# Modulation weights queued at once, four projection banks, background pieces in turn and spaced, casts of the second norm deferred

## The chip, the cores and the metric

The kernel runs on the 8 cores of one Trainium2 chip. Each core works on one batch element; the cores exchange nothing. The metric is the device time in microseconds of the slowest core.

## The reference

One adaLN block: a modulation from `c`, attention over 2048 tokens with 16 heads of 64, and a gated feed-forward with quantised activations and ternary weights. For one batch element:

```python
mod = silu(c) @ wmod                       # 6 vectors of 1024: sa, ca, ga, sb, cb, gb
ga = sign(ga) * max(|ga|, 0.25); gb likewise
h = layernorm(x) * (1 + ca) + sa
x = x + ga * attention(h, W_qkv)
h = layernorm(x) * (1 + cb) + sb
x = x + gb * ffn(h)
# ffn(h) = bit(silu(bit(h, w_gate)) * bit(h, w_up), w_down)
# bit(x, w) = quant127_per_token(x) @ ternary(w), with
# ternary(w) = clip(round(w / mean|w|), -1, 1) * mean|w|
```

Every core has all weights to load and to make ternary itself: w_gate, w_up and w_down are 16 MB each in float32, and each is read twice, once for the mean of |w| and once for the ternary values.

## The kernel before

Each engine has a `Lane`, which runs its instructions in the order of the program text; `need` puts a wait in front of the next one. Loads and stores go out on SyncE's queue (`Y`), except the first constants (ScalarE) and the attention weights (`load_wqk`, `load_wv`, on GpSimd). `V` is VectorE, `S` ScalarE (ACT), `G` GpSimd (POOL).

**Start.** Five constants are loaded on ScalarE's queue, and V, S, PE and G all wait for the last of them. x comes in 16 tiles of 128 tokens, in four blocks n of four. `mod_load(k)` loads a tile of the modulation matrix into one of six buffers, `mod_dot(k)` multiplies it with silu(c) on V and sums it into a column of `modv`; the first 16 columns give `modv` and `avec` (lines 519 to 528). For each block, `stats(n)` takes mean and variance on V, with a square root on S; `normalize(n)` scales on S (block 0) or G; `turn(n)` transposes eight times four tiles on PE into the banks of `psS`, which S (five of eight) and V (three) evacuate into `hA` with scale and bias. `project(n)` makes K of the first head pair and V of the first two: jobs of 8 or 16 matmuls into a bank of `psP`, then a square on S, casts on V, and a small matmul for the norms (lines 531 to 544). `take_bank` hands out the two banks of `psP`.

**Attention.** 512 steps (loop at line 1028): group g of 16 steps is one head pair (c = g // 4) against 512 queries (q = g % 4). A step makes scores (`emit_scores`), their exponentials (`emit_exp`, 128x1024 on S) and, some steps later, the products with V (`emit_av`). `queue_group` adds the projections of the next group or head pair as jobs; `run_jobs` spreads their matmuls over the steps, and a job waits until `BANK_GAP` = 4 steps after the older bank's last end. Odd c below 7 have V projections too. At the end of a group `finish_group`, `divide` and `add_residual` run on V; PE's next group waits for the division at line 743.

**Background.** `bg` holds pieces: `piece_mean(m, k)` loads 128x1024 of a weight matrix (m = 0 gate, 1 up, 2 down) into one of four buffers `stg` and sums |w| on V (line 577); `piece_tern(m, k)` loads it again, scales and clips on G (lines 597, 600) and casts to fp8, on V in attention and on S from step 512 on (lines 618, 621); `piece_mod(k)` is one more dot product. `job_scale(m)` turns the sums into a scale with one small matmul. `bg_tick` is called once a step: it runs the parts that are due (none while a group is being finished), and starts the next piece when it has a credit, fewer than four are under way and the next buffer is free. Order: means of 0 and 1, modulation, ternary 0 and 1, means of 2, ternary 2. The ternary gate and up stay in `tg` and `tu`; that of down goes to the tensor `td` in memory, from which `dt8` is loaded.

**Behind attention.** `norm2_stages(g, wide)` is the second norm with quantisation for 256 tokens, a list of stages; the list for g = 0 runs one stage a step from step 464 on, once no job is left (line 1050). Its first stage loads x2n, stages `cast(0)` and on need it. `emit_A(g)` is the gate and up pass over 16 pairs of tiles: 16 matmuls for the gate, 16 for up, three V and two S instructions; after each pair a hook runs `rate` stages of the next norm and one `bg_tick`. `emit_C(g)` is the down pass. The order is A(0), A(1), C(0), A(2), C(1) and so on.

## Time and profile before

| | us |
|---|---|
| median of the runs shown | 1600.59 |
| profiled execution | 1589.67 |
| its span, slowest core (6) | 1588.1 |
| PE busy | 1392.0 (88%) |
| VectorE busy | 1122.2 (71%) |
| ScalarE busy | 1013.6 (64%) |
| GpSimd busy | 377.9 (24%) |

The spans of the eight cores run from 1579.0 to 1588.1 us. Busy time of PE counts a matmul from start to modelled end, with overlaps taken once; it says that something is on the engine, not that it runs at its peak. The stages matter more than these sums: the start lasts to 128.8 us, attention to 826.6, and from 987.4 on the feed-forward runs in the steady order.

### The profile page before, as it was taken

Reading aid. Unit: us, or ns where it says so; the run is one execution under the profiler, and the core shown is the slowest. Engines: PE = TensorE matmul, PEld = TensorE weight load, DVE = VectorE, ACT = ScalarE, POOL = GpSimd, SP = SyncE. Lnnn points to the kernel's source line nnn. Section 1 sums busy time; section 2 is a strip of 40 time slices with the busy share of each in tenths; the row PEclk is TensorE's granted clock in tenths of the full one; section 3 lists DMA queues with packets and bytes.
Section 4 is the critical chain, followed back from the end, with each engine's and each line's share of the span. In section 5 each row is a group of like instructions: output and inputs, shape, how many; then the busy total and the mean of one; then the engine's idle time right before and its main releaser. Section 6 shows DMA issues by size and latency. Waiting matters only on the chain.

```text
span 1588.1 us, 28129 instructions; the slowest of 8 cores (1579.0 to 1588.1 us)
## 1 busy us (share of the span) xinstructions
PE 1392.0 (88%) x9640; PEld 955.0 (60%) x9702; DVE 1122.2 (71%) x1803; ACT 1013.6 (64%) x1313; POOL 377.9 (24%) x341
## 2 busy tenths in 40 slices
PE   0368989999999899989688596999999999999997
PEld 0243334433544344433247485888898888889885
DVE  3757778788766666578696968768686777777561
ACT  2126867788778777878747378665657475655451
POOL 5411000000336666551026533101000010101011
PEclk9688999999999999999889898999999999999999
DMA  9904655656445545446526355604132140505043
GB/s 244 326 4 146 197 188 161 211 186 225 160 146 168 170 128 158 159 150 218 190 99 183 118 158 159 187 1 142 46 93 95 46 142 13 174 1 160 1 139 115
DMA packets 88364, 222.76 MB, mean 140 GB/s; under 512 B 8480, under 2 KB 37408, under 8 KB 88224
## 3 DMA queue, kind: packets, MB, share of 16 engines
q1 hardware_dynamic: 85776, 214.47, 42.1%
q0 software_dynamic: 1728, 6.29, 2.2%
q8 instruction: 80, 1.31, 0.3%
q14 instruction: 60, 0.49, 0.1%
q10 hardware_dynamic: 720, 0.20, 0.1%
HBM read 206.24 MB, written 20.97 MB: 143 GB/s over the span
## 4 chain that ended last, share of the span: by engine, by line
PE 63%; DVE 18%; DMA 6%; issue 6%; ACT 4%; POOL 2%; DVEq 0%; ACTq 0%; POOLq 0%; SPq 0%
PE psS L1133 13%; PE psV L1264 12%; PE psS L1141 12%; PE psV L747 9%; PE psS L728 8%; PE psP L329 3%; PE psP L391 3%; DVE Dt L759 2%; DVE Dt L767 2%; DMA stg<-wu 2%; DVE macc L577 1%; DMA stg<-wg 1%; DMA wm<-wmodT 1%; DVE Rt L771 1%; DMA b_swap<-bswap 1%
## 5 line engine op out<-in xcount | busy, mean ns | idle before, releaser
L735 ACT ACTIVATE PT<-psS 128x1024 bf16<-128x1024 f32 x512 | 504.4, 1025 | 145.5 <-PE psS L728 140.5
L728 PE MATMUL psS<-Qz,Kz 128*128 128x512 bf16 x989 | 302.3, 385 | 33.4 <-ACT PT L735 25.4
L747 PE MATMUL psV<-PT,Vt 128*128 128x512 bf16 x1006 | 285.2, 384 | 25.5 <-DVE Rt L771 24.3
L1133 PE MATMUL psS<-hq,tg 128*128 128x256 bf16 x2048 | 247.8, 275 | 10.6 <-DVE hq L962 7.3
L1141 PE MATMUL psS<-hq,tu 128*128 128x256 bf16 x2048 | 246.5, 274 | 10.6 <-DVE gup L1107 10.6
L1264 PE MATMUL psV<-gq,dt 128*128 128x256 bf16 x2048 | 234.2, 276 | 17.5 <-DMA dt<-td 12.3
L1264 PEld LDWEIGHTS psV<-gq,dt 128*128 128x128 fp8e4 x2048 | 201.9, 99 | 44.5 <-issue 19.5
L1133 PEld LDWEIGHTS psS<-hq,tg 128*128 128x128 fp8e4 x2048 | 201.7, 99 | 36.0 <-issue 11.4
L1141 PEld LDWEIGHTS psS<-hq,tu 128*128 128x128 fp8e4 x2048 | 200.8, 98 | 36.8 <-issue 12.6
L728 PEld LDWEIGHTS psS<-Qz,Kz 128*128 128x128 bf16 x1024 | 93.2, 98 | 166.3 <-issue 90.3
L747 PEld LDWEIGHTS psV<-PT,Vt 128*128 128x128 bf16 x1024 | 99.8, 99 | 151.6 <-issue 38.4
L1147 DVE TENSOR_TENSOR sg<-psS,alB 128x512 f32<-128x512 f32 x128 | 88.2, 689 | 130.0 <-PE psS L1133 127.4
L1282 POOL TENSOR_TENSOR xo<-xo,ot 128x512 f32<-128x512 f32 x32 | 42.6, 1331 | 564.4 <-DVE ot L1276 564.4
L1152 ACT ACTIVATE sg<-sg 128x512 f32<-128x512 f32 x128 | 79.9, 625 | 149.0 <-DVE sg L1147 148.6
L329 PE MATMUL psP<-hA,wqk 128*128 128x512 bf16 x504 | 147.1, 387 | 5.9 <-DVE Kz L339 2.9
L1219 ACT ACTIVATE vq<-vq,cst_s 128x512 f32<-128x512 f32 x128 | 91.3, 713 | 85.4 <-DVE vq L1214 84.7
L597 POOL TENSOR_SCALAR stg<-stg,mstat 128x1024 f32<-128x1024 f32 x96 | 120.3, 1254 | 102.2 <-DMA stg<-wd 58.1
L375 POOL TENSOR_SCALAR Qz<-yrt,nkm 1x512 bf16<-1x512 f32 x32 | 25.8, 806 | 442.2 <-DVE yrt L369 442.2
L577 DVE TENSOR_REDUCE macc<-stg 128x1 f32<-128x1024 f32 x96 | 113.6, 1213 | 15.0 <-DMA stg<-wg 6.3
L1214 DVE TENSOR_TENSOR vq<-gup,s2B 128x512 f32<-128x512 f32 x128 | 98.0, 772 | 17.3 <-ACT gq L1221 17.1
L600 POOL TENSOR_SCALAR stg<-stg 128x1024 f32<-128x1024 f32 x96 | 106.1, 1105 | 15.9 <-POOL stg L597 15.3
L1221 ACT ACTIVATE gq<-vq,cst_s 128x512 bf16<-128x512 f32 x128 | 92.4, 722 | 12.4 <-ACT vq L1219 0.7
(130 smaller groups left out, 1569.8 us busy)
## 6 DMA issues: line engine op xcount, KB each, us to landing
stg<-wg SPq DMA_DIRECT2D x64, 512.0 KB, 5.0
stg<-wu SPq DMA_DIRECT2D x64, 512.0 KB, 4.9
stg<-wd SPq DMA_DIRECT2D x64, 512.0 KB, 4.5
dt<-td SPq DMA_DIRECT2D x64, 512.0 KB, 4.6
wm<-wmodT SPq DMA_DIRECT2D x48, 512.0 KB, 8.1
xin<-x SPq DMA_DIRECT2D x16, 512.0 KB, 13.0
xr<-xT SPq DMA_DIRECT2D x32, 256.0 KB, 3.1
x2d<-xr SPq DMA_DIRECT2D x32, 256.0 KB, 2.0
```

What stands on the lines that cost most here:

```text
L329: return PE.e.matmul(bank, wt[:, (w * 8 + i) * 128:(w * 8 + i + 1) * 128], hA[:, i * T + n * 512:i * T + (n + 1) * 512], start=(i == 0), s ...
L577: st_free[b] = mean_tok[m] = V.did(V.e.reduce_sum(macc[:, m * 32 + k:m * 32 + k + 1], stg[b], axis=AX, apply_absolute_value=True))
L597: t = G.did(G.e.tensor_scalar(stg[b], stg[b], mstat[:, 4 * m + 1:4 * m + 2], RND, ALU.mult, ALU.add))
L600: st["p1"] = tern_row[0] = G.did(G.e.tensor_scalar(stg[b], stg[b], RND + 1.0, RND - 1.0, ALU.min, ALU.max))
L728: ins = PE.e.matmul(bankS(2 * b + hd), Kz[c % 2][hd][:, kt * 128:(kt + 1) * 128], Qz[g % 3][hd], start=True, stop=True)
L735: exp_tok[s] = s_free[b] = S.did(S.e.activation(PT[s % NPT], psS[:, b * 1024:(b + 1) * 1024], AF.Exp, scale=0.125))
L747: ins = PE.e.matmul((psA, psD)[hd], Vt[c % 3][:, vo:vo + 128], PT[s % NPT][:, hd * 512:(hd + 1) * 512], start=(kt == 0), stop=(kt == 15))
L1133: ins = PE.e.matmul(bankS(b)[:, o_ * 256:(o_ + 1) * 256], tg[:, w:w + 128], hq[g % 2][:, db * 256:(db + 1) * 256], start=(db == 0), stop=( ...
L1141: ins = PE.e.matmul(bankS(2 + b)[:, o_ * 256:(o_ + 1) * 256], tu[:, w:w + 128], hq[g % 2][:, db * 256:(db + 1) * 256], start=(db == 0), st ...
L1214: t = V.did(V.e.tensor_tensor(vq[b].rearrange("p (o t) -> p o t", o=2), gb[:, i * 512:(i + 1) * 512].rearrange("p (o t) -> p o t", o=2), b ...
L1221: ff["vq"][b] = gq_tok[(g, i)] = S.did(S.e.activation(gqb[:, i * 1024:i * 1024 + 512], vq[b], AF.Identity, bias=cst[:, 2:3]))
L1264: ins = PE.e.matmul(bank[:, k * 256:(k + 1) * 256], dt8[wb][:, oc * 128:(oc + 1) * 128], gqb[:, (oc // 2) * 1024 + (oc % 2) * 256: (oc // ...
```

## The change

- Sixteen buffers for modulation tiles instead of six, so the first 16 are all issued ahead; x tiles 4 to 15 are issued right behind them, three of the constants on SyncE's queue between x tiles 7 and 8. Only two constants are loaded on ScalarE's queue, and only S and PE wait for them at the start. `load_wqk(1)` moves behind the memsets, wqk(0) and wv(0) ahead of all but the first memset.
- Up to the first attention step the projections take turns over four banks: the two of `psP`, and `psA` and `psD`.
- `turn(0)` to `turn(2)` are evacuated by ScalarE alone, and `project(0)` stands behind `stats(2)` and `normalize(2)`.
- `bg`: means of 0, modulation, then for m = 0 and 1 ternary tiles of m and means of m + 1 in turn, then ternary 2. A piece starts every second step at the earliest, without credits, with parts 6 and 9 steps after the start (before 9 and 12); none starts in steps 470 to 511.
- `norm2_stages(0, True)` has nine empty stages between load and first cast, five before.
- Three stages of the norm per hook in A(0), two before.

```diff
@@ -123,7 +123,8 @@
     tu = at("tu", o + 32, [128, 32768], FP8)
     xin = [at("xin%d" % i, (o, o, 145, 173)[i // 4] + 16 * (i // 4 == 1) + 4 * (i % 4),
               [128, 1024], F32) for i in range(16)]
-    wm = [at("wm%d" % i, o + 32 + 4 * i, [128, 1024], F32) for i in range(6)]
+    wm = [at("wm%d" % i, o + 32 + 4 * i if i < 6 else 67 + 4 * (i - 6) if i < 14 else
+             (189, 199)[i - 14], [128, 1024], F32) for i in range(16)]
     cB = at("cB", o + 56, [128, 1024], F32)
     mjunk = at("mjunk", o + 60, [128, 1024], F32)
     o = 67
@@ -187,34 +188,38 @@
         return psS[:, i * 512:(i + 1) * 512]
 
     def bankP(i):
+        if i > 1:
+            return (psA, psD)[i - 2]
         return psP[:, i * 512:(i + 1) * 512]
 
...
-    f_c = Flow(nc, "const")
-    for dst, src in [(cst, cst_d), (ident, identf_d), (onesf, onesf_d), (onesb, onesb_d),
-                     (bswap, bswap_d)]:
+    f_c, f_c2 = Flow(nc, "const"), Flow(nc, "const2")
+    for dst, src in [(cst, cst_d), (ident, identf_d)]:
         t_const = f_c.go(S, dst, src)
-    for lane in (V, S, PE, G):
-        lane.need(t_const)
-
-
-    f_wm = [Flow(nc, "wm%d" % i) for i in range(6)]
-    wm_free = [None] * 6
+    S.need(t_const)
+    PE.need(t_const)
+
+
+    f_wm = [Flow(nc, "wm%d" % i) for i in range(16)]
+    wm_free = [None] * 16
     wm_tok = {}
     modt = {}
 
+    def wm_slot(k):
+        return k if k < 16 else k % 6
+
     def mod_load(k):
-        b = k % 6
+        b = wm_slot(k)
         Y.need(wm_free[b])
         wm_tok[k] = f_wm[b].go(Y, wm[b], wmod_d[k * 128:(k + 1) * 128, :])
 
     mj, t_silc = {"t": None}, [None]
 
     def mod_dot(k):
-        b = k % 6
+        b = wm_slot(k)
         V.need(wm_tok[k], t_silc[0], mj["t"])
         t = V.did(V.e.scalar_tensor_tensor(mjunk, wm[b], 1.0, cB, ALU.mult, ALU.mult,
                                            accum_out=modv[:, k:k + 1]))
@@ -239,14 +244,18 @@
     gate_vec_t = [None]
 
 
-    p_free = [None, None]
-    p_end = [-9, -9]
+    p_free = [None] * 4
+    p_end = [-9] * 4
     now = [0]
     p_order = []
+    p_wide = [True, 0, 1, 2, 3]
     p_one = [False]
 
     def take_bank(b=None):
-        if b is None:
+        if p_wide[0]:
+            p_wide.append(p_wide.pop(1))
+            b = p_wide[-1]
+        elif b is None:
             b = 1 if p_one[0] or p_end[1] < p_end[0] else 0
         PE.need(p_free[b])
         return b
@@ -267,7 +276,7 @@
             if job_state["cur"] is None:
                 if not jobs:
                     return used
-                if budget < 1e6 and now[0] - min(p_end) < BANK_GAP:
+                if budget < 1e6 and now[0] - min(p_end[:2]) < BANK_GAP:
                     return used
                 n, needs, mm, after = jobs.popleft()
                 needs()
@@ -406,10 +415,10 @@
             return t
         job(16, needs, mm, after, 8.0)
 
+    G.did(G.e.memset(Vt[0], 1.0))
     load_wqk(0)
     load_wv(0)
-    load_wqk(1)
-    for i in range(3):
+    for i in range(1, 3):
         G.did(G.e.memset(Vt[i], 1.0))
     for i in range(3):
         for h in range(2):
@@ -432,8 +441,14 @@
     for t in range(4):
         x_load(t)
     t_cB = Flow(nc, "cB").go(Y, cB, bass.AP(c_d.tensor, 0, [[0, 128], [1, D]]))
-    for k in range(6):
+    for k in range(16):
         mod_load(k)
+    for t in range(4, 8):
+        x_load(t)
+    for dst, src in [(onesb, onesb_d), (bswap, bswap_d), (onesf, onesf_d)]:
+        t_const2 = f_c2.go(Y, dst, src)
+    for t in range(8, 16):
+        x_load(t)
     S.need(t_cB)
     t_silc[0] = S.did(S.e.activation(cB, cB, AF.Silu))
     bankS_free = [None] * 4
@@ -485,7 +500,7 @@
...
-            if db % 2 or db == 4:
+            if db in on_act[n]:
...
     turned, ready = {}, {}
+    on_act = (range(8), range(8), range(8), (1, 3, 4, 5, 7))
 
     def project(n):
         PE.need(*ready[n])
         norm_k = job_qk(0, 1, n)
         if n:
+            PE.need(t_const2)
             norms.pop()()
         job_v(0, 2 * n)
         if n < 3:
@@ -519,21 +536,17 @@
     normalize(0)
     for k in range(16):
         mod_dot(k)
-        if k < 10:
-            mod_load(k + 6)
-        elif k == 10:
-            for t in range(4, 16):
-                x_load(t)
     V.need(modt[15])
     t_avec = V.did(V.e.tensor_scalar(avec, modv[:, 8:16], 1.0, None, ALU.add))
     for k in range(16, 22):
         mod_load(k)
+    load_wqk(1)
     turn(0)
     stats(1)
     normalize(1)
-    project(0)
     stats(2)
     normalize(2)
+    project(0)
     turn(1)
     stats(3)
     normalize(3)
@@ -542,6 +555,9 @@
     turn(3)
     project(2)
     project(3)
+    p_wide[0] = False
+    PE.need(t_const2)
+    V.need(t_const, t_const2)
     x_done = turned[3]
 
     LAST = 32 * 16
@@ -665,26 +681,25 @@
 
     vb_tok = [None]
     gv_tok = {}
-    for m in range(2):
-        for k in range(32):
-            bg.append(piece_mean(m, k))
+
+    for k in range(32):
+        bg.append(piece_mean(0, k))
     bg.append((lambda: None, [lambda: sum_rows(0), lambda: job_scale(0)]))
     for k in range(24, 48):
         bg.append(piece_mod(k))
-    bg.append((lambda: None, [lambda: sum_rows(1), vec_b, lambda: job_scale(1)]))
-    for m in range(2):
+    bg.append((lambda: None, [vec_b]))
+    for m in range(3):
         for k in range(32):
             bg.append(piece_tern(m, k))
-    for k in range(32):
-        bg.append(piece_mean(2, k))
-    bg.append((lambda: None, [lambda: sum_rows(2), lambda: job_scale(2)]))
-    for k in range(32):
-        bg.append(piece_tern(2, k))
+            if m < 2:
+                bg.append(piece_mean(m + 1, k))
+        if m < 2:
+            bg.append((lambda: None, [lambda m=m: sum_rows(m + 1), lambda m=m: job_scale(m + 1)]))
     later = deque()
     rest, rest_end = deque(), [-9]
-    under, credit, ahead = [0], [0], [7]
-
-    def bg_tick(step, start=None):
+    under, next_start = [0], [0]
+
+    def bg_tick(step, lead):
 
         quiet = not rest and step > rest_end[0] + 1
         for _ in range(len(later)):
@@ -693,16 +708,15 @@
                 under[0] -= last
             else:
                 later.append((when, part, last))
-        if start:
-            credit[0] += 1
-            ahead[0] = start
-        if credit[0] and bg and under[0] < 4 and not st_held[st_n[0] % 4]:
-            credit[0] -= 1
+        if LAST - 42 <= step < LAST:
+            return
+        if bg and under[0] < 4 and step >= next_start[0] and not st_held[st_n[0] % 4]:
+            next_start[0] = step + (2 if len(bg[0][1]) < 2 else 2)
             under[0] += 1
             load, parts = bg.popleft()
             load()
             for i, part in enumerate(parts):
-                later.append((step + ahead[0] + 3 * i, part, i == len(parts) - 1))
+                later.append((step + lead + 3 * i, part, i == len(parts) - 1))
 
 
     f_xr = [Flow(nc, "xr%d" % i) for i in range(2)]
@@ -740,7 +754,7 @@
         g, kt = s // 16, s % 16
         c = g // 4
         if kt == 0:
-            PE.need(av_free[0])
+            PE.need(av_free[0], p_free[2], p_free[3])
         PE.need(exp_tok[s], v_tok[(c, kt // 2)])
         for hd in range(2):
             vo = (kt * 2 + hd) * 128
@@ -971,7 +985,7 @@
 
         wait = lambda: None
         if wide:
-            return ([load, wait, wait, wait, wait, wait, cast(0), cast(1), wait,
+            return ([load] + [wait] * (9 if g == 0 else 5) + [cast(0), cast(1), wait,
                      both(stat(0), cast(2)), both(stat(1), cast(3)), wait, stat(2), stat(3), wait,
                      var, root, recip] +
                     [both(times(j), minus(j)) for j in range(4)] +
@@ -1054,7 +1068,7 @@
                 side.extend(norm2_stages(0, True))
             if side:
                 side.popleft()()
-        bg_tick(s, 9 if (s % 16) in ((0, 2, 4, 7, 9, 11, 13) if s < 470 else ()) else None)
+        bg_tick(s, 6)
         step += 1
     while rest:
         rest.popleft()()
@@ -1294,7 +1308,7 @@
         run_side(rate[0])
         if bg or later:
             hook_n[0] += 3
-            bg_tick(step + hook_n[0], 4 if bg else None)
+            bg_tick(step + hook_n[0], 4)
             run_jobs(1e9)
 
     hook_n = [0]
@@ -1307,7 +1321,7 @@
         return nxt
 
     side.extend(norm2_stages(1, True))
-    rate = [2]
+    rate = [3]
     emit_A(0, hook_A)
     rate[0] = 1
     drain(side)
```

## Rows read from the trace of the kernel before

**Rows 1.** Start in stages: length; busy PE, PEld, DVE, ACT, POOL; PEclk, DMA, GB/s

```profile
4.00:16.00 12.00, 0.00 (x0) 0.00 (x0) 0.00 (x0) 0.00 (x0) 0.00 (x0) 1.00 0.95 235
16.00:48.00 32.00, 3.64 (x16) 3.27 (x16) 21.88 (x39) 8.56 (x8) 28.93 (x20) 0.85 1.01 290
48.00:79.00 31.00, 15.06 (x83) 11.39 (x84) 22.46 (x48) 7.09 (x12) 8.05 (x8) 0.72 1.01 326
79.00:127.00 48.00, 30.84 (x201) 22.61 (x203) 26.57 (x52) 11.34 (x17) 8.04 (x7) 0.89 0.02 6
```

**Rows 2.** Timeline of the start: start, length, engine, line, instruction, idle before it

```profile
4.03 39.85 SPq L58 DMA_DIRECT2D wm<-wmodT  x16
...
51.39 1.23 DVE L219 SCALAR_TENSOR_TENSOR mjunk<-wm,cB 128x1024 f32<-128x1024 f32 x1 [0.46 <-DMA wm<-wmodT]
...
52.73 0.17 DVE L528 TENSOR_SCALAR avec<-modv 128x8 f32<-128x8 f32 x1
```

**Rows 3.** Timeline, from the statistics of block 3 to the first scores

```profile
86.62 0.30 ACT L456 ACTIVATE rstd<-bnm,cst_s 128x4 f32<-128x4 f32 x1 [5.67 <-DVE bnm L451]
...
96.73 3.65 PE L391 MATMUL psP<-wv,hA 128*128 128x256 bf16 x32 [2.13 <-DVE Kz L339]
...
128.81 1.86 PE L728 MATMUL psS<-Qz,Kz 128*128 128x512 bf16 x4 [4.32 <-POOL Qz L378]
```

**Rows 4.** Stages of attention: three chunks of four groups each, then the last three groups

```profile
220.30:311.40 91.10, 85.94 (x448) 43.55 (x456) 73.63 (x95) 66.79 (x73) 6.58 (x10) 1.00 0.56 173
391.10:481.20 90.10, 85.35 (x449) 43.95 (x456) 63.74 (x102) 66.68 (x73) 32.51 (x29) 1.00 0.43 147
561.20:651.60 90.40, 85.91 (x448) 43.36 (x454) 57.18 (x88) 66.47 (x73) 55.62 (x52) 1.00 0.49 151
751.80:827.70 75.90, 53.79 (x223) 22.45 (x228) 58.75 (x79) 50.75 (x57) 11.52 (x10) 0.87 0.49 161
```

**Rows 5.** Timeline around the second norm's load and the end of attention

```profile
762.63 0.38 SPq L58 DMA_DIRECT2D x2n<-x2d  x1
...
773.01 0.63 ACT L813 ACTIVATE lb<-x2n 128x512 bf16<-128x512 f32 x1 [6.59 <-DMA x2n<-x2d]
...
809.38 1.01 PE L747 MATMUL psV<-PT,Vt 128*128 128x512 bf16 x2 [4.10 <-DVE Rt L771]
...
826.44 1.91 PE L1133 MATMUL psS<-hq,tg 128*128 128x256 bf16 x16
...
836.97 3.30 PE L1133 MATMUL psS<-hq,tg 128*128 128x256 bf16 x16 [3.24 <-DVE mstat L651]
```

**Rows 6.** Stages of A(0) and of a later stretch, and timeline rows between

```profile
826.40:911.90 85.50, 63.62 (x541) 54.12 (x540) 66.59 (x111) 43.91 (x60) 46.31 (x38) 0.92 0.46 139
...
911.94 3.57 PE L1133 MATMUL psS<-hq,tg 128*128 128x256 bf16 x16 [7.03 <-DVE hq L962]
...
987.37 7.24 PE L1264 MATMUL psV<-gq,dt 128*128 128x256 bf16 x48 [12.28 <-DMA dt<-td]
...
1100.00:1150.00 50.00, 50.00 (x461) 44.81 (x459) 35.96 (x59) 36.25 (x56) 2.54 (x2) 1.00 0.28 91
```

**Rows 7.** Groups by line, shapes apart: busy us, mean ns of one, idle before

```profile
L1147 DVE TENSOR_TENSOR sg<-psS,alB 128x512 f32<-128x512 f32 x128 | 88.2, 689 | 130.0 <-PE psS L1133 127.4 <-DMA x2d<-xr 1.7
...
L618 ACT ACTIVATE tdo<-stg,cst_s 128x1024 fp8e4<-128x1024 f32 x32 | 36.3, 1134 | 1.0 <-POOL stg L600 1.0
...
L577 DVE TENSOR_REDUCE macc<-stg 128x1 f32<-128x1024 f32 x96 | 113.6, 1213 | 15.0 <-DMA stg<-wg 6.3 <-DMA stg<-wd 4.0 <-DMA stg<-wu 3.9
...
L490 ACT ACTIVATE hA<-psS,modv,avec 128x512 bf16<-128x512 f32 x20 | 14.9, 773 | 34.5 <-DVE avec L528 22.2 <-PE psS L484 12.0
```

**Rows 8.** Landing of stg loads, 180 to 200 and 600 to 700 us; timeline, group's end

```profile
DMA to landing us min/median/max: 4.3/8.1/10.9
...
DMA to landing us min/median/max: 3.4/4.3/5.5
...
204.01 1.01 PE L747 MATMUL psV<-PT,Vt 128*128 128x512 bf16 x2 [4.84 <-DVE Rt L771]
```

## Prediction

> **What bounds the kernel now.** I read three things in order: the table of stages, then the rows of time inside each stage that is not dense, then the groups by line for prices. The reader should see four stretches.
>
> Start, 0 to 128.8 us: the 16 DMA engines are full from 4 to 79 us and idle afterwards, while PE does only 49.6 us of work in the 123 us shown [rows 1]. The last of the 16 dot products of modulation starts at 51.39 behind its load, and `avec` is there at 52.73 [rows 2]. From there a serial walk goes on: ACT waits 5.67 us for the statistics of block 3 of x, PE waits 2.13 us for a square and two casts before it gets a projection bank, and the first scores come at 128.81 [rows 3].
>
> Attention, 128.8 to 826.6: for three chunks of four groups with V projections the time is 91.1, 90.1 and 90.4 us, with PE busy 85 to 86 of them and Vector at 73.6, 63.7 and 57.2 [rows 4]. The three have different background work (means only, modulation, ternary tiles), so its kind hardly matters there; PE sets the pace. The last three groups are different: 75.9 us with PE at 53.8 and ACT at 50.8, neither full [rows 4].
>
> From the end of attention to the first down-projection, 826.6 to 987.4: A(0), the first up and gate pass, takes until 911.94, 85.5 us for 16 pairs of gate and up tile of 32 matmuls each, which at the later pace of 461 matmuls in 50 us are 3.5 us a pair and 56 in all; A(1) ends 63.2 us later, at 975.1, and PE waits 12.28 us for `dt` [rows 5, 6]. After that PE has hardly a gap, and the change doesn't touch it.
>
> **The change, part by part.**
>
> *Weights of modulation queued at once, fewer constants waited for.* The issue of 16 loads was stretched over 39.85 us, since only six buffers existed [rows 2]. But the DMA engines were full all the time [rows 1], so only the order of bytes can gain. Before `avec` the kernel must load 4 tiles of x, cB, 16 tiles of weights, wqk(0), wv and wqk(1) (Pool issues it behind its memsets, still well before the end): 24 tiles of 0.52 MB, 12.6. The rows moved 12 x 0.235 + 32 x 0.290 = 12.1 MB from 4 to 48. So the last weight tile could land at 49, and it landed at about 51.3, because loads of x ran beside it [rows 1, 2]. Now more loads queue behind it than before, so some of this stays. I take 2 us (0 to 3): `avec` at 50.7. That Vector no longer waits for the constants is worth nothing by itself: its dots end behind their loads, and this covers some ten microseconds of earlier start. In a sentence apart: the Trainium skill, page "DMA: Bandwidth & Descriptors", section "Issuing engines are not separate DMA queues", says that transfers of all issuing engines interleave on the same 16 engines; by it alone the weights gain nothing from being queued early and this term is 0. The full share of 1.01 agrees.
>
> *Turns of blocks 0 to 2 on ACT alone, project(0) behind stats(2).* Eight evacuations x 0.77 = 6 us a block [rows 7], much as long as now, but Vector is free to go on. The new walk: stats(1) ends at about 57.5 (x tile 7 lands at about 56: 2.1 MB after the weights at 0.326 MB/us [rows 1]); stats(2) at 64 (x tile 11 at 62.5); the square, casts and V copies of project(0), twice PE's 2.13, to 68.2; stats(3), which took the 5.67 that ACT waited and a little more, to 74.2 [rows 3]. So the square root of block 3 is at 74.3, where it is at 86.62 now [rows 3]. That is 33.9 us after `avec` now and 23.6 then: 10.3 us. If x lands 3 us later this falls by 3.
>
> *Four banks for projections.* From the root at 86.62 to the first scores takes 42.2 us now [rows 3]. Each of projects 1 to 3 waits once for the casts (2.13) and once more for V's copies or the norm. With psA and psD as third and fourth bank, PE runs project(1) in 8 (the clock is low there), turn(3) in 4, project(2) in 5.7, and project(3) down to the scores in 13, after 4 us in which turn(2) is evacuated: 34.7 us, a gain of 7.5 (4 to 9). First scores at 128.8 - 2 - 10.3 - 7.5 = 109. Start in all: 20, bounds 11 to 25.
>
> *Background order and spacing.* Before, seven starts in 16 steps with nine steps of lead; now one every two steps with six, at most four under way. A mean holds its buffer 6 steps and a ternary tile 9, and nothing runs in 3 steps of 16 around a group's end. By counting, the first 32 means and 24 dots end at about step 118, and each alternating run of 64 takes some 171 steps (6 and 6 in 32): 290, 461. Four ternary tiles of wd fit before step 470, so 28 stay for after attention; now it is all 32 (every one ran on ACT [rows 7]). Costs: 96 means x 1.213 on Vector are unchanged, four ternary casts more, none dearer than a mean: 5 us at most on Vector, which is not the bound. Since three kinds of load gave 90.1 to 91.1, I take 0, cover being Vector's idle 17 to 33 us of 90 [rows 4]. Without that cover they cost their 5. The shorter lead is 6 x 1.36 = 8 us against a landing of 4.3 us in the quiet and 8.1 in the crowded stretch [rows 8]: some waits near the start, so bounds from 8 lost to 3 gained. Apart: the Trainium skill, page "SBUF — State Buffer", section "Who interferes with whom", says that DVE in a two-port mode, or with two SBUF inputs against a reading GpSimd op, waits for GpSimd's whole instruction, and a tensor_reduce never does; so means beside ternary work are the harmless pairing and the term would be 0 or better.
>
> *Nothing started in steps 470 to 511, casts deferred.* Of the 75.9 us of the last three groups ACT, the fullest but Vector, worked 50.8, the floor [rows 4]. The x2n load issued at 762.63 landed at 773.01 and ACT stood 6.59 us before its cast; PE stood 4.10 for Vector at 809.38 [rows 5]. Four more empty steps are 4.4 us, and without stg loads beside it the x2n load lands sooner: the 6.6 goes. About 17 means, 20 us of the 58.8 of Vector, go from this stretch [rows 4, 7], and with them most of the 4.1. GpSimd's chain of eight ops of the norm stays, and Vector waits for it in order. So 75.9 - 6.6 - 3.4 = 66, a gain of 10 (5 to 14).
>
> *What is late next.* The job of scale(2) now falls at step 472 and the bank gap pushes the last norm of Q, and with it the norm's start, from 472 to 475; with four more stages the last stage is at 475 + 41 = 516, past the last step 513. So `spread` and `scale` run behind the last group's division: hq(0) is ready about 11 us after the last AV: the division, for which PE waited 4.84 elsewhere [rows 8], and ten more Vector ops of at most 0.69 [rows 7]. Now PE starts A(0) at once (826.44) but, two tiles on, stands until 836.97, 10.4 us after [rows 5]. Then it starts at 11 with nothing done: 7 us of matmul lost.
>
> *Rate 3 in A(0).* 38 stages at two a hook are 19 hooks, but A(0) has 16; six stages run after it, and PE waits 7.03 us for hq(1) [rows 6]. At three they end in hook 13. A(0)'s Vector work: busy 66.6 of the 85.5 us [rows 6], of which 16 pairs x 3 ops x 0.69 = 33, the last group and mean 10, so the norm 23. It gets heavy at hook 5, when PE has done six pairs, 11 + 21 = 32 us after the last AV; left are 23 + 10.5 x 2.1 + 2 for the root = 47, to 79, and PE ends its tiles about 3 before. So A(1) begins at 76 against 85.3 (911.9 - 826.6): gain 9 (2 to 13), the 7 lost already in it.
>
> *After A(0).* No slow clock at A(1)'s first tiles (3.57 for 16 matmuls, at the later pace 1.74 [rows 6]): 2. The last ternary tile is 3 hooks earlier (28 for 31), 3 x 3.5 = 10 us, so `dt` is there; what is left is the quantised input, freed of three to four ACT casts of 1.13 [rows 7]: 4 (1 to 7).
>
> **Sum.** 20 + 0 + 10 + 9 + 2 + 4 = 45. The profiled execution took 1589.7 (span 1588.1, 1.6 around it), so 1545 by its own clock; the median of the shown runs is 1600.6, 11 above it, so 1556.
>
> **Rivals.**
> A, *the DMA engines bound the start anyway.* For: full to 79 us [rows 1]. Against: 76 us of the start lie behind `avec`, and the engines' loads are over 50 us before its end. If x lands 8 us late in stats(1) to (3), the start gives 12: 1564. The skill's rule above is its reason.
> B, *the deferral only moves the wait.* For: hq(0) comes 11 us late, PE's clock falls (16 matmuls in 3.57 after such a gap), A(0) is Vector-bound. If A(0) regains nothing (0 for 9) and the last groups give 5: 1570.
> C, *the shorter lead.* Vector and Pool work in order, so a mean that waits for its load holds the casts and the division behind it, and PE waits for both. Where the median landing was 8.1 us, at 8 us the lead is just gone [rows 8]. PE waited 4.84 us at the end of a group there [rows 8]. It decides from 10 of the 29 groups (48 us: no gain left); with all of them it is 140 us and 1696, slower. Against: in the rest landing is near half the lead.
>
> **How the numbers follow.** Forecast 0.62, A 0.15, B 0.17, C 0.06. About 2% (32 us, the line at 1568.6) is what a measurement of this kernel tells from no change. The forecast lies on the faster side for 0.58 and within for 0.04; A 0.11 and 0.04; B 0.05 and 0.12; C 0.02 within and 0.04 slower. Faster 0.74, same 0.22, slower 0.04. The range takes A and B in and the high bounds of start, last groups and A(0) in part: 1536 to 1582.
>
> **What would show it.** First scores near 109 (A: 117); `avec` near 50.7; chunks of four groups still at 90 to 91; the last three groups at 66; first tile of A(0) about 11 us behind the last AV and A(1) at 76 behind it; no wait on `dt`; 28 ternary casts on ACT. I am wrong if the groups themselves get slower, most likely with DVE or POOL waiting for stg, or if the ACT-only turns hold PE longer than 6 us a block.

## The result, and the profile after

The changed kernel takes 1590.1 us (median of all executions), the kernel before 1599.6: ratio 0.994, 95% interval 0.9917 to 0.9963. It is 10 us faster, not 45; within 2%, and above the predicted range of 1536 to 1582. (Some executions run up to 12% longer, with the cores of a die at a lower granted clock; the ratios, and the times given further down, leave them out.) The profiled execution took 1600.5 (span 1598.9, core 1) and is the longest of those compared, while that of the kernel before, 1589.7, is shorter than the others of its kernel. So the two profiles overstate what was lost; by how much is worked out below.

The start, in the timeline of core 1 (columns as in [rows 2]):

```profile
52.20 0.17 DVE L540 TENSOR_SCALAR avec<-modv 128x8 f32<-128x8 f32 x1
...
76.19 0.30 ACT L471 ACTIVATE rstd<-bnm,cst_s 128x4 f32<-128x4 f32 x1 [3.75 <-DVE bnm L466]
...
109.70 1.86 PE L742 MATMUL psS<-Qz,Kz 128*128 128x512 bf16 x4 [5.09 <-POOL Qz L387]
```

Against [rows 2, 3]: `avec` 0.5 us earlier, the root of block 3 10.4, the first scores 19.1 (128.81 to 109.70). These are core 6 before and core 1 now; in the mean over the eight cores `avec` stands at 51.9 before and 52.1 now, so it gains nothing, and the first scores at 128.9 and 108.8. The start as a whole did what was forecast.

Attention in stages of the same core (columns as in [rows 4]); each stage runs from one group's end to that of the fourth behind it:

```profile
134.98:238.22 103.24, 83.31 (x362) 35.23 (x360) 74.59 (x94) 66.52 (x73) 6.00 (x9) 0.93 0.65 188
238.22:332.56 94.34, 86.25 (x429) 41.45 (x428) 72.02 (x112) 66.71 (x72) 19.38 (x20) 0.98 0.57 181
...
596.34:682.62 86.28, 82.71 (x424) 40.28 (x423) 63.18 (x88) 66.61 (x73) 33.41 (x33) 1.00 0.51 168
...
761.23:831.47 70.24, 54.50 (x219) 21.04 (x218) 38.99 (x57) 52.42 (x59) 25.34 (x21) 0.88 0.20 64
```

The first stage is 103.24 us long, with VectorE, ScalarE and GpSimd hardly busier than in the kernel before, where core 6 needed:

```profile
153.76:242.70 88.94, 79.09 (x357) 34.85 (x363) 69.21 (x83) 66.54 (x73) 6.00 (x9) 0.96 0.61 190
```

From group 1 to 28 the changed kernel takes 606 to 626 us on its cores, the one before 591 to 598. Here most of the start's gain went, and slower groups are the first sign of being wrong that the prediction names. The waits of core 1 from 135 to 761 us (us in total, times, longest) say behind what:

```profile
POOL stg L613 <- DMA stg<-wg: 64.8, 29, 8.7
POOL stg L613 <- DMA stg<-wu: 53.6, 25, 7.0
...
DVE macc L593 <- DMA stg<-wu: 30.4, 16, 5.6
...
PE psV L761 <- DVE Rt L785: 24.4, 15, 4.4
...
DVE macc L593 <- DMA stg<-wd: 19.4, 10, 7.4
...
DVE macc L593 <- DMA stg<-wg: 17.3, 5, 6.6
```

VectorE's means wait 67.1 us for their loads; in the kernel before, on core 6 from 154 to 752 us, it was 10.6, and 10.2 of it stand in two rows:

```profile
DVE macc L577 <- DMA stg<-wg: 6.3, 4, 2.7
...
DVE macc L577 <- DMA stg<-wu: 3.9, 4, 1.9
```

One chain of such a wait, in the timeline of core 2; first SyncE's queue, then the engines:

```profile
130.35 2.91 SPq L58 DMA_DIRECT2D stg<-wg  x2
139.60 0.33 SPq L58 DMA_DIRECT2D x2d<-xr  x1
142.06 0.33 SPq L58 DMA_DIRECT2D xr<-xT  x1
142.80 15.42 SPq L58 DMA_DIRECT2D stg<-wg  x8
```

```profile
151.05 1.22 DVE L593 TENSOR_REDUCE macc<-stg 128x1 f32<-128x1024 f32 x1 [5.29 <-DMA stg<-wg]
152.31 0.69 DVE L378 TENSOR_SCALAR yrt<-psP 128x512 int32<-128x512 int32 x1
...
153.22 0.69 POOL L384 TENSOR_SCALAR Qz<-yrt,nkm 1x512 bf16<-1x512 f32 x1 [22.29 <-DVE yrt L378]
154.08 0.69 POOL L387 TENSOR_SCALAR Qz<-yrt,nkm 1x512 bf16<-1x512 f32 x1 [0.17 <-POOL Qz L384]
...
154.91 1.01 PE L742 MATMUL psS<-Qz,Kz 128*128 128x512 bf16 x2 [5.24 <-POOL Qz L387]
```

The mean at 151.05 waits 5.29 us for its load, which was issued at 142.80 and landed 8.2 us later. It was also issued late: SyncE's queue took nothing from 133.26 to 139.60, because the store of the residual `x2d` stood at its head and `xr` was not yet there (it is made at the group's end), and from 139.93 to 141.98 the reload of `xr` waited for that store to land. Then four loads of `stg` went out within 1.6 us. Behind it on VectorE stands the root `yrt` for the norm of Q; behind that GpSimd's two ops, and behind those the next group's scores: PE waits 5.24 us. The two matmuls then take 1.01 us where two take 0.59 elsewhere in this stage: the granted clock is 0.50 from 154.9 to 160 us, where it was 1.00 from 144 to 149. Rival C's chain, as it was described; the stall of the queue ahead of it was not in the prediction. Its own waits on core 2 from 135 to 715 us (total, times, longest):

```profile
SPq L46 <- DVE xr L793: 214.6, 26, 13.9
...
SPq L46 <- DMA x2d<-xr: 54.2, 26, 4.0
```

Between the ends of groups 0 and 28 core 2 has 31 waits of over 0.5 us of a mean for its load, 74 us in all. Every one is for a load issued within 5 us behind a wait for such a store to land. The kernel before has the same two waits (core 6: 210.4 and 50.7 us); with nine steps of lead its means wait the 10.6 us above.

Behind attention, core 1 (the last product with V ends at 831.37):

```profile
841.89 0.37 SPq L58 DMA_DIRECT2D x2n<-x2d  x1
...
841.96 3.57 PE L1147 MATMUL psS<-hq,tg 128*128 128x256 bf16 x16 [9.71 <-DVE gtmp L233]
...
989.93 4.83 PE L1278 MATMUL psV<-gq,dt 128*128 128x256 bf16 x22 [4.60 <-DMA dt<-td]
...
996.57 0.38 PE L1278 MATMUL psV<-gq,dt 128*128 128x256 bf16 x2 [1.05 <-ACT gq L1235]
```

A(0) starts 10.6 us behind the last product, as forecast; A(1) starts at 922.5, 91 behind it (85.3 before, 76 forecast); `dt` costs 4.6 instead of 12.3 [rows 6], after which PE waits several times for the quantised input.

### The profile page after: what moved, and what is told of

Its sections match the earlier page's. It is cut to its first block, busy times and chain, and to the rows that moved or that the text cites. A ratio compares the mean times of both kernels' runs of the same rounds, so it can differ in the third digit from the quotient of the medians.

```text
span 1598.9 us, 28123 instructions; the slowest of 8 cores (1576.9 to 1598.9 us)
## 1 busy us (share of the span) xinstructions
PE 1413.7 (88%) x9702; PEld 959.1 (60%) x9702; DVE 1115.0 (70%) x1798; ACT 1014.9 (63%) x1318; POOL 374.4 (23%) x341
## 4 chain that ended last, share of the span: by engine, by line
PE 60%; DVE 17%; DMA 9%; issue 6%; SPq 4%; ACT 3%; POOL 1%; DVEq 0%; POOLq 0%; ACTq 0%
PE psS L1147 12%; PE psV L1278 12%; PE psS L1155 12%; PE psV L761 8%; PE psS L742 7%; SPq L58 3%; DMA stg<-wu 3%; PE psP L338 2%; PE psP L400 2%; DVE Dt L773 2%; DVE Dt L781 2%; DMA stg<-wg 2%; DMA x2d<-xr 2%; DMA wm<-wmodT 1%; DVE Rt L785 1%
## 5 line engine op out<-in xcount | busy, mean ns | idle before, releaser
L742 PE MATMUL psS<-Qz,Kz 128*128 128x512 bf16 x1024 | 314.9, 391 | 28.8 <-ACT PT L749 17.0
L761 PE MATMUL psV<-PT,Vt 128*128 128x512 bf16 x1024 | 292.4, 389 | 29.7 <-DVE Rt L785 29.7
L1278 PE MATMUL psV<-gq,dt 128*128 128x256 bf16 x2048 | 237.5, 277 | 14.0 <-ACT gq L1235 9.4
L1147 PEld LDWEIGHTS psS<-hq,tg 128*128 128x128 fp8e4 x2048 | 201.5, 98 | 34.9 <-issue 10.4
L613 POOL TENSOR_SCALAR stg<-stg,mstat 128x1024 f32<-128x1024 f32 x96 | 116.8, 1216 | 220.0 <-DMA stg<-wd 89.8
L338 PE MATMUL psP<-hA,wqk 128*128 128x512 bf16 x480 | 141.0, 388 | 4.6 <-DVE Kz L348 3.5
(145 smaller groups left out, 1576.3 us busy)
```

The source lines that it names most:

```text
L338: return PE.e.matmul(bank, wt[:, (w * 8 + i) * 128:(w * 8 + i + 1) * 128], hA[:, i * T + n * 512:i * T + (n + 1) * 512], start=(i == 0), s ...
L613: t = G.did(G.e.tensor_scalar(stg[b], stg[b], mstat[:, 4 * m + 1:4 * m + 2], RND, ALU.mult, ALU.add))
L742: ins = PE.e.matmul(bankS(2 * b + hd), Kz[c % 2][hd][:, kt * 128:(kt + 1) * 128], Qz[g % 3][hd], start=True, stop=True)
L761: ins = PE.e.matmul((psA, psD)[hd], Vt[c % 3][:, vo:vo + 128], PT[s % NPT][:, hd * 512:(hd + 1) * 512], start=(kt == 0), stop=(kt == 15))
L1147: ins = PE.e.matmul(bankS(b)[:, o_ * 256:(o_ + 1) * 256], tg[:, w:w + 128], hq[g % 2][:, db * 256:(db + 1) * 256], start=(db == 0), stop=( ...
L1278: ins = PE.e.matmul(bank[:, k * 256:(k + 1) * 256], dt8[wb][:, oc * 128:(oc + 1) * 128], gqb[:, (oc // 2) * 1024 + (oc % 2) * 256: (oc // ...
```

## The experiments

All kernels in one table. Each figure is the mean over the eight cores of the profiled execution: the end of group 0 (start of its first transpose `Dt<-psV`), the time from there to the end of group 28, from there to the end of group 31, and what follows to the end of the span. The ratio is that of the times to those of the kernel before, with its 95% interval; where a time stands instead, there was one execution to go by.

| kernel | group 0 ends | groups 1–28 | last three | behind | ratio |
|---|---|---|---|---|---|
| before | 153.5 | 594.2 | 74.3 | 761.4 | 1 |
| changed | 134.3 | 615.5 | 69.9 | 767.1 | 0.994 (0.992–0.996) |
| start only | 132.2 | 598.0 | 74.5 | 762.8 | 0.986 (0.984–0.989) |
| old background | 133.1 | 596.5 | 71.8 | 761.8 | 0.984 (0.982–0.987) |
| new order, old pace | 132.6 | 582.8 | 71.7 | 798.4 | 1.002 (1.000–1.003) |
| old order, new pace | 132.6 | 648.0 | 70.9 | 755.4 | 1.015 (1.012–1.017) |
| new order, old pace, lead 6 | 132.8 | 627.1 | 82.1 | 756.3 | 1.007 (1.004–1.010) |
| changed, lead 8 | 133.1 | 584.6 | 67.7 | 806.2 | 1600.5 us |
| changed, small loads | 132.9 | 582.7 | 69.9 | 766.3 | 1561.3 us |
| changed, no deferral | 133.8 | 605.5 | 78.4 | 756.0 | 0.992 (0.991–0.994) |
| changed, stop at 462 | 133.7 | 610.4 | 65.3 | 765.9 | 0.995 (0.992–0.998) |
| start only, rate 3 | 132.6 | 595.9 | 74.1 | 757.8 | 0.988 (0.979–0.996) |
| lead 8, gap 2 | 134.1 | 605.3 | 72.6 | 762.2 | 0.991 (0.989–0.994) |
| old background, lead 8, gap 2 | 133.2 | 618.4 | 85.3 | 749.4 | 0.998 (0.996–0.999) |
| start only, two banks | 144.1 | 596.0 | 73.8 | 762.0 | 1587.1 us |
| start only, early project(0) | 141.3 | 595.6 | 74.2 | 761.9 | 1584.0 us |
| lead 8, two a pair | 133.2 | 581.4 | 67.7 | 785.9 | 0.990 (0.987–0.993) |
| lead 7, two a pair | 131.9 | 590.3 | 66.8 | 767.3 | 0.980 (0.978–0.983) |
| new order, old pace, two a pair | 132.6 | 583.8 | 72.9 | 767.3 | 0.981 (0.978–0.984) |
| the same, no deferral | 132.1 | 583.0 | 78.0 | 761.8 | 0.983 (0.978–0.988) |

Two of these, "no deferral" and "stop at 462", run the changed kernel's own code up to step 461, and their groups took 605.5 and 610.4. The five kernels with the background of before and the new start have 595.6 to 598.0, 596.4 in the mean. So against the background of before the changed kernel loses 9 to 19 us in its groups, from run to run.

The groups don't all hold the same work. Loads into `stg` issued between the ends of groups 0 and 28: 138 in the kernel before and with its background; 154 in the changed kernel, without deferral and with small loads (153 with the stop at 462); with the new order 132 at the old pace and 160 at the old pattern with lead 6; 138 with lead 8, 147 to 149 with lead 7; 169 with the old order at the new pace; 149 and 158 in the two kernels with gap 2.

**Start, pace and order.** First the start alone, the changed kernel with background, deferral and rate of before:

```diff
-            return ([load] + [wait] * (9 if g == 0 else 5) + [cast(0), cast(1), wait,
+            return ([load] + [wait] * (5 if g == 0 else 5) + [cast(0), cast(1), wait,
-    rate = [3]
+    rate = [2]
```

(`bg` and `bg_tick` as in the kernel before.)

> The kernel before with the changed start alone (sixteen weight buffers, four banks, turns on ACT, later project(0)); the background's order and pace, the five empty stages and two stages a hook are those of before. The changed kernel reaches its first group's end 17 to 23 us earlier, but its groups 1 to 28 take 9 to 36 us more than before. If the background (pace or order) costs those, this kernel keeps the start's 20 us: about 1580, ratio 0.987, groups 1 to 28 at 591 to 598 us. If the earlier start itself stretches attention, whatever the background (all loads of eight cores fall together differently), the groups take 600 or more here too and the time is 1590 to 1595.

Measured: 1576.3 us, groups 598.0 (595 to 603). The start keeps its 21 us; the background costs most of them in the changed kernel.

The same with nine empty stages and rate 3:

> The changed kernel with the background's order and pace of before (credits, nine steps of lead, no stop at 470); the nine empty stages and three stages a hook stay. Against the start alone it tells what the deferral and the rate are worth. If the deferral and the rate are worth what was forecast for them (10 + 9 less the 17 means that go on beside the last groups), it is some 10 us under the start alone: 1570. If the late hq(0) eats them, as the changed kernel's 205.9 to 198.8 us from last product with V to A(2) suggests (193.4 before), it is level with the start alone or up to 5 us slower: 1578 to 1585.

(The figure 205.9 in it is a slip; the changed kernel's is 198.8.) Ratio 0.984 against 0.986: the last groups give 2.7 us, what follows 1.0, and the intervals overlap. Then order and pace crossed; the pace of before in the new order (`bg_tick` again as in the kernel before):

```diff
-        bg_tick(s, 6)
+        bg_tick(s, 9 if (s % 16) in ((0, 2, 4, 7, 9, 11, 13) if s < 470 else ()) else None)
```

> The changed kernel's order of pieces (means of 0, modulation, then ternary and means in turn) with the pace of before: seven starts in 16 steps, nine steps of lead, no stop at 470. Theory 1 (the shorter lead and the spacing cost the groups): attention is back, groups 1 to 28 at 591 to 598 us, the time 1575 to 1582. Theory 2 (ternary tiles and means in turn cost it, by two kinds of load and two engines on four buffers): groups at 605 to 625 us, the time about 1590.

and the new pace with the old list of pieces:

> The changed kernel with the order of pieces of before, but its own pace: one start every two steps, six steps of lead, none in steps 470 to 511. Theory 1 (lead and spacing): groups 1 to 28 at 605 to 625 us, the time about 1590. Theory 2 (order): groups at 591 to 598 us, the time 1575 to 1582. If both cost a part, this and the kernel with new order and old pace lie between, at about 1585 each.

New order with old pace has the groups at 582.8, new pace with old order at 648.0, over the 605 to 625 expected. So the pace costs them and the order does not: at the same pace the new order takes 14 us less than the old (582.8 for 596.5), with VectorE waiting some 23 us for GpSimd instead of some 30. The gain isn't only a matter of fewer pieces, since the kernel with small loads (below) has 154 loads for 138 and 582.7 us; what makes it isn't shown. In time the first kernel missed its 1575 to 1582 us (ratio 1.002), for it pays behind attention: 36 pieces were left, the scale of matrix 2 came late, and PE waits for `dt`:

```profile
PE psV L1279 <- DMA dt<-td: 42.9, 2, 40.3
```

**Lead or pattern.** The pace has two parts. Eight steps of lead in the changed kernel, and six in the pattern of before:

> The changed kernel with eight steps of lead for six; a start every second step, order and stop as changed. Only attention is to be read: fewer pieces end in it, about 41 are left for behind it, so dt comes late and the whole time is over 1600. If the lead costs the groups, groups 1 to 28 are at 577 to 592 us as with the pace of before, and VectorE's waits for stg are under 20 us; if the pattern (a start every second step) costs them, they stay at 605 or more.

> The changed kernel's order with the start pattern of before (seven in 16 steps, credits) but six steps of lead; about 14 ternary tiles of the last matrix are left for behind attention. If the lead alone costs the groups: groups 1 to 28 at 605 or more, and the time 1585 to 1595. If the pattern costs them: 577 to 592 and, since dt is ready in time, a time of 1560 to 1570, under every kernel so far.

Six steps of lead cost in either pattern (627.1 against 582.8; the time, 1607.7, is over what either theory said), eight in the new one cost nothing (584.6). That speaks for the lead and against the pattern. But these pairs alone don't part the lead from the amount of work, since a shorter lead frees the buffers sooner and lets more loads into the groups (160 for 132, 154 for 138); the small loads below do. And VectorE's waits were not under the 20 us expected at eight steps; they are 34.7 in all on core 0:

```profile
DVE macc L593 <- DMA stg<-wu: 19.3, 7, 5.0
...
DVE macc L593 <- DMA stg<-wd: 8.6, 5, 3.8
...
DVE macc L593 <- DMA stg<-wg: 6.8, 4, 3.2
```

So a wait of this kind is not paid one for one; VectorE has idle time to put it in. Seven steps, with two starts a pair behind attention (below):

> The changed kernel with seven steps of lead and two starts a pair behind attention. Groups 1 to 28 took 605 to 615 us at six steps (three profiled executions) and 581 to 585 at eight. If the cost sets in only where the lead falls under the landing plus the time by which the buffers come free late, seven steps lie near eight: 584 to 592. If it grows evenly with each step taken away: 595 to 600. Some 31 pieces instead of 41 are left behind attention, so the rest is 765 to 775 instead of 786; time 1560 to 1572 in the first case, 1575 to 1582 in the second.

Groups at 590.3 (587 to 594): 583 at eight, 590 at seven, 605 to 616 at six. The cost grows faster than the lead shrinks, as in the first of the two cases expected.

**Landing, or engines.** Is it the late load or the number of operations? All loads into `stg` but the first four bring 64 columns:

```diff
-            st["t"] = f_st[b].go(Y, stg[b], src[:, k * 1024:(k + 1) * 1024])
+            w = 1024 if st_n[0] <= 4 else 64
+            st["t"] = f_st[b].go(Y, stg[b][:, :w], src[:, k * 1024:k * 1024 + w])
```

> The changed kernel in which all loads of weight tiles into stg but the first four bring only 64 of 1024 columns; every VectorE, GpSimd and ScalarE operation stays. It leaves out most of the weights (means and ternary values are of old data). The loads land sooner, so: if late landing behind a six-step lead is what costs attention, groups 1 to 28 fall from 606 to 626 to 575 to 590 us. If it is two engines meeting on the same memory or the number of operations in a group, they stay over 600.

582.7 us with every operation in place and all 154 loads issued. Landings of `stg` from 400 to 580 us, in the changed kernel and then in this one, and this one's waits:

```profile
DMA to landing us min/median/max: 3.5/6.2/10.6
```

```profile
DMA to landing us min/median/max: 1.6/2.2/4.4
...
DVE macc L594 <- DMA stg<-wd: 1.8, 1, 1.8
DVE macc L594 <- DMA stg<-wu: 0.8, 1, 0.8
```

The late landing is the cause, and neither the number of operations nor two engines on the same memory. (The kernel with new order and old pace has full loads, 132 of them, and the same 582.8 us, so it isn't the traffic as such.) The median of 6.2 lies under the 8.2 us of six steps; the upper end does not, and the lead has to cover the load's time in SyncE's queue as well. That time is the same with small loads (core 3: 240.5 us of waits for `xr`), which land soon enough behind it. No run takes the residual off this queue.

**Buffers.** `stg` is held for lead + 3 steps by a ternary tile. With eight steps, two between its parts, and a stop at 476, no deferral:

```diff
-                later.append((step + lead + 3 * i, part, i == len(parts) - 1))
+                later.append((step + lead + 2 * i, part, i == len(parts) - 1))
```

> The changed kernel with eight steps of lead, two steps instead of three between the two parts of a ternary tile (so that a buffer is held 10 steps, not 11), no start in steps 476 to 511 instead of 470 to 511, and five empty stages. If the lead is what costs the groups and the deferral what costs behind attention: groups 1 to 28 at 582 to 592 us (before: 594, changed: 616 in the profiled execution), the rest behind attention at 756 to 764, time 1555 to 1570, under every kernel so far. If the shorter gap makes VectorE wait for GpSimd instead, the groups are at 600 or more and the time at 1575 or more.

> The start changed, order and start pattern of before, but eight steps of lead for nine and two steps between the parts of a ternary tile; five empty stages, three stages a hook. More pieces end inside attention: about 13 ternary tiles are left for 32. If eight steps are enough, groups 1 to 28 stay at 595 to 603 and the rest behind attention falls from 762 to 756 (as in the kernels with 18 tiles left or fewer): time 1565 to 1572. If the edge already lies between eight and nine steps in this order (many pieces in a row of one kind, up to four under way), the groups are at 610 or more and the time at 1580 or more.

The second has the background of before, with the same lead and gap. Both lost: 605.3 and 618.4. VectorE hardly waits for loads of means now (10.8 us on core 4 of the first), but for GpSimd, whose two operations end too late for a cast two steps on. First the changed kernel's core 1, then this one's core 4:

```profile
DVE tu L637 <- POOL stg L616: 4.2, 4, 2.9
...
DVE tg L637 <- POOL stg L616: 0.7, 1, 0.7
```

```profile
DVE tg L637 <- POOL stg L616: 29.7, 10, 4.4
...
DVE tu L637 <- POOL stg L616: 23.4, 10, 4.3
```

The same chain, with another slack taken away. The old order's 648.0 at the new pace has both: on the slowest core VectorE waited 32.5 us for loads of means, 52.8 for GpSimd (17.8 of it before casts of the last matrix) and 6.1 for stores of `td`. Its groups also hold fifteen ternary tiles more than the changed kernel's. How the 32 us between the two kernels fall to these isn't settled.

**The last three groups.** The changed kernel without its four extra empty stages:

```diff
-            return ([load] + [wait] * (9 if g == 0 else 5) + [cast(0), cast(1), wait,
+            return ([load] + [wait] * (5 if g == 0 else 5) + [cast(0), cast(1), wait,
```

> The changed kernel with five empty stages instead of nine before the first cast of the second norm; all else as changed. If the deferral only moves the wait: hq(0) is ready earlier, the first tile of A(0) starts about 2 us behind the last product with V instead of 10.6, the last three groups take 73 instead of 70, and the time stays at 1588 to 1592. If the deferral pays, as forecast, through the last groups: it is 4 to 8 us slower. If it is only a loss through the late hq(0): it is 3 to 7 us faster, 1583 to 1587.

78.4 us for the last groups, 8.5 more than with the deferral (73 were expected), and 4 more than in the kernel before, although no piece is started beside them; behind attention 11.1 us less. Two things make the norm late. Its load is handed out at step 475 instead of 472, as the prediction says under "What is late next": without the deferral ScalarE has begun 482 exponentials before the first cast, in the kernel before 479. Three steps are some 4 us. The rest is in SyncE's queue. The kernel before issues the load 10.9 us behind the end of group 28 (751.75 to 762.63, [rows 5]); in the changed kernel (core 1, group 28 ends at 761.23):

```profile
774.54 6.15 SPq L58 DMA_DIRECT2D td<-tdo  x3
...
780.85 0.38 SPq L58 DMA_DIRECT2D x2n<-x2d  x1
...
786.58 0.63 ACT L827 ACTIVATE lb<-x2n 128x512 bf16<-128x512 f32 x1 [2.98 <-DMA x2n<-x2d]
```

Three stores of ternary tiles stand ahead of it, each waiting for its cast: the load goes out 19.6 us behind the end of group 28, 8.7 later than before, of which some 4 are the later step. The four empty stages only make up for both. A stop eight steps earlier (`LAST - 50`):

> The changed kernel with no start in steps 462 to 511 instead of 470 to 511, so that no ternary tile of the last matrix falls into attention and no store of one stands in SyncE's queue ahead of the second norm's load. If those stores are what kept the load late (issued 19.6 us behind the end of group 28 in the changed kernel, 10.9 before): it is issued at some 11, no wait of ScalarE for it, and the last three groups take 65 to 67 us for 69.9; behind attention 32 tiles are left, which costs 3 to 8 us there, so the time is 1588 to 1594. If the load is late for another reason, the last three groups stay at 69 to 71.

Last groups 65.3 us, as expected, though not by the whole of the mechanism: two stores still stand ahead of the load, which goes out 16.7 us behind the end of group 28 (753.15), 5.8 later than before, some 4 of it again the later step. That is just early enough; ScalarE waits 0.56 for it:

```profile
766.46 3.22 SPq L58 DMA_DIRECT2D td<-tdo  x2
769.84 0.38 SPq L58 DMA_DIRECT2D x2n<-x2d  x1
...
776.09 0.63 ACT L827 ACTIVATE lb<-x2n 128x512 bf16<-128x512 f32 x1 [0.56 <-DMA x2n<-x2d]
```

No time is gained in all (0.995); the 4.6 us are less than the groups before them vary, and the rest stays at 765.9, where 3 to 8 us more were expected for 32 tiles left (30 were cast behind attention).

**Rate.** The start alone, with three stages a hook:

> The start changed, background of before, five empty stages, three stages a hook in A(0) (the kernel with the start alone has two, the one with the deferral nine empty stages and three). The forecast gave rate and hq(0) together 9 us. If the rate alone is worth the gap before A(1) (7 us in the kernel before): the rest is at 754 to 758 us against 762.8, the time 1568 to 1572. If A(0) is bound by VectorE, so that the stages only come earlier and push the gate and up work back: rest 761 to 764, time 1576.

The rest falls from 762.8 to 757.8: with hq(0) in time, rate 3 is worth 5 us in this pair of profiles, as forecast; the times, 1570.1 for 1576.3, agree, though one of the four executions took 1586.8.

**The start's parts.** Two banks (`p_wide` false from the beginning), and `project(0)` ahead of `stats(2)` with turns shared by ScalarE and VectorE:

> The kernel with the changed start alone, but projections before the first step take turns over two banks, as before. The forecast gave four banks 7.5 us (4 to 9): the end of the first group then falls back from 132.2 us (mean of the cores) to 136 to 141. If the walk to the root of block 3 and not the banks sets the first scores, it stays at 132 to 134.

> The kernel with the changed start alone, but project(0) ahead of stats(2) and the turns shared by ACT and VectorE as before. The forecast gave this step 10.3 us together with the weights queued at once: the end of the first group falls back from 132.2 to 139 to 142 us, and the root of block 3 from 76 to some 83 us. If the gain came from the earlier loads of x alone, both stay within 2 us.

Group 0 ends 11.9 us later with two banks (144.1, where 136 to 141 was expected) and 9.1 with the early project(0). First scores and root of block 3 on the slowest cores, two banks and then early project:

```profile
79.62 0.30 ACT L471 ACTIVATE rstd<-bnm,cst_s 128x4 f32<-128x4 f32 x1 [0.67 <-DVE bnm L466]
...
119.51 1.87 PE L745 MATMUL psS<-Qz,Kz 128*128 128x512 bf16 x4 [4.33 <-POOL Qz L387]
```

```profile
83.93 0.30 ACT L471 ACTIVATE rstd<-bnm,cst_s 128x4 f32<-128x4 f32 x1 [5.37 <-DVE bnm L466]
...
117.82 1.87 PE L745 MATMUL psS<-Qz,Kz 128*128 128x512 bf16 x4 [5.09 <-POOL Qz L387]
```

**Keeping both gains.** New order and old pace had the shortest groups and a late `dt`. Two calls of `bg_tick` at each pair of A(0) and A(1), in that kernel and in the changed one with lead 8:

> New order with the pace of before (groups 1 to 28 at 582.8 us, but 798 us behind attention, since dt came 41 us late), now with two calls of bg_tick at each pair of A(0) and A(1). If the ternary tiles behind attention are held back by one start a pair and not by GpSimd or ScalarE, dt is some 25 to 35 us earlier, the rest 765 to 772 us and the time 1560 to 1567, under every kernel so far. If the four buffers or GpSimd hold them back, the rest stays over 785 and the time at 1585 or more.

> The changed kernel with eight steps of lead and two starts at each pair in A(0) and A(1). With eight steps alone the groups took 584.6 us, the last three 67.7, the rest 806. By the same reasoning as in the kernel with new order, pace of before and two a pair: the rest falls by 25 to 35 to 771 to 781 and the time is 1564 to 1574; 1595 or more if buffers or GpSimd are the limit.

The first gives 1565.6 us; its wait for `dt` is 8.5 us (42.9 without). The second keeps 26.7 of it and misses its 771 to 781 by 5: 41 pieces were left there. Lead 7 with two a pair, whose expectation stands above, gave 1565.7. The first without deferral:

> New order, pace of before, two starts a pair, and five empty stages for nine. Against the same kernel with nine stages (last three groups 72.9, rest 767.3) it tells what the deferral does where no store of a ternary tile stands ahead of the norm's load. If the deferral is a trade of a wait in attention for one behind it, the last three groups are 2 to 4 us longer and the rest 4 to 10 shorter, the time 1560 to 1566. If it is a pure gain or loss: 1570, or 1555.

Last groups 5.1 longer, the rest 5.5 shorter: an even trade. Its time, 1569.6, isn't the 1560 to 1566 expected of a trade, but not told apart from the 1565.6 with deferral. The two best, lead 7 and new order with old pace, both with two a pair, are 2.0 and 1.9% under the kernel before and some 1.3% under the changed one.

## Why the prediction was wrong

*Start, 20 us: right.* 19.2 at the end of group 0, as a mean over the cores. Within it, on the two cores compared, `avec` gave 0.5 for 2 (nothing in the mean over the cores); the walk to the root 9.9 for 10.3 (86.62 - 52.73 to 76.19 - 52.20); the banks from root to first scores 8.7 for 7.5 (42.2 to 33.5). Taken back alone, the banks cost 11.9 at the end of group 0, since with two of them the root is 3 us later as well. The Trainium skill, page "DMA: Bandwidth & Descriptors", section "Issuing engines are not separate DMA queues", says that transfers of all issuing engines interleave on the same 16 engines, which gave 0 for the weights; the means of 51.9 and 52.1 us for `avec` agree with it. (Two slips in the working: PE's work in [rows 1] adds up to 49.5 us, not 49.6, and the upper bounds of the three terms, 3, 10.3 and 9, make 22 and not 25.)

Of the forecast's 45 us some 35 are missing. 9 to 19 are lost in the groups, 5.6 in the last three, and 20.7 behind attention, where 9 + 2 + 4 were expected and 5.7 were lost.

*Background, 0 us, bounds 8 lost and 3 gained: the first step that failed.* It cost 9 to 19 us in groups 1 to 28. That is a difference of two effects: against the new order with its loads in time (582.7) the short lead cost 23 to 33 us, and the new order gave some 14 back. I named the mechanism (rival C) and put it at the edge: "at 8 us the lead is just gone" where the median landing was 8.1, and "in the rest landing is near half the lead". Two things were missing. The lead is counted from the step at which a piece is handed out, not from the issue of its load, and SyncE's queue also carries the residual: at each group's end it stands until `xr` is made and until its store has landed (214.6 and 54.2 us on core 2), and loads handed out meanwhile go out late and together. And a load must land in nearly all cases, not in the median one: 3.5 to 10.6 us around a median of 6.2. My own bound was also inconsistent: C at 48 us for 10 groups in the rivals, 8 us in the term's range, and nothing between, though the 23 to 33 us of the lead are what five to seven of 29 groups would give. "Its kind hardly matters" did not hold: at the old pace the new order's groups are 14 us shorter. The Trainium skill, page "SBUF — State Buffer", section "Who interferes with whom", by which a `tensor_reduce` never waits for GpSimd and means beside ternary work are harmless, agrees with 582.7 and 582.8 us.

*Last three groups, 10 us: 4.4.* The size was near what there was to win (9.0 with the stop at 462), but the sum said "without stg loads beside it the x2n load lands sooner" and had not asked what the four ternary tiles that now fit before step 470 bring with them: three stores in the queue ahead of that load. I had counted the four, and priced them at four casts. The three steps by which the norm starts later I had seen too, but they stand in no term of this sum.

*A(0) to A(1), 9 us: the second step that failed, -6 (91 for 76).* The first tile at 11 us was right. hq(1) was ready at 84.5 us behind the last product for 79 forecast. Wrong is "PE ends its tiles about 3 before": the norm ends in hook 13, and pairs 14 to 16 come behind that. Its stages, and VectorE's load with them, fall on the second half:

```profile
841.96:882.00 40.04, 36.14 (x288) 30.24 (x288) 21.30 (x35) 21.24 (x30) 14.16 (x12) 0.88 0.42 136
882.00:922.52 40.52, 30.77 (x250) 25.54 (x251) 37.13 (x63) 18.74 (x26) 17.54 (x14) 0.92 0.37 114
```

VectorE is busy 21 of the first 40 us and 37 of the next 40.5. The norm's first stage, the load of `x2n`, can't go out before hq(0) has left that buffer: issued at 841.89. So the late hq(0) delays twice, and rival B had the mechanism: the rest is 11.1 us shorter without the deferral, and the deferral moves a wait. (B's A(0) was to regain nothing; it lost 6.) With hq(0) in time the rate gave 5. That leaves some 10 of the 20.7 us for the pairs behind the norm and for C(0)'s input, which no run separates.

*Slow clock at A(1), 2 us: moved, not gained.* A(1)'s first 16 matmuls take 1.91 us now, but the same 3.57 us is at the first tile of A(0), after its 9.71 us of idling.

*`dt`, 4 us:* its wait fell by 7.7 (12.28 to 4.60), and PE then waited for the quantised input instead. From the last product with V to A(2) it is 198.8 us, 193.4 before.

*Sum:* 19 - (9 to 19) + 4 - 6 (the rest, 761.4 to 767.1) is -2 to 8; measured 10 (6 to 13 by the interval). The profiles are single executions, and their groups alone differ by 10 us.

## What to carry to other kernels

A prefetch's lead has to be read against the late end of its landings and against the queue that issues it: if that queue stands behind a store whose data comes at the end of a chain, every load handed out meanwhile goes out late, and one step of lead (1.4 us here) was worth 6 to 25 us. A kernel with a longer lead may be quicker also because it does less in the same stretch; count the pieces before comparing. Before a piece of background work is allowed into a stretch, list every instruction that it puts on every in-order queue, its stores too, and look which load stands behind them. A deferred start in front of a serial chain is a trade until it is shown that the chain's end is not waited for.

## What the runs showed that I had not expected

The load waits of VectorE are not paid one for one: 34.7 us of them with lead 8 left the groups as short as the 2.6 us with small loads did. The same code up to step 461 took 605.5, 610.4 and 615.5 us in three profiled executions, a spread of 10, while the six kernels in the new order with eight or nine steps of lead (and three between the parts of a tile) or with small loads agree within 3.2 us (581.4 to 584.6): in these executions a short lead made the time not only longer but uncertain. And the largest of SyncE's waits in attention, for the residual at each group's end, is in the kernel before as well; moving it to another queue is the next thing to try, and no run here did.
